# The first step of a state-space mixer, reordered: both row loads ahead of x's blocks, slot 4 ahead of the third scores, late step widths and softplus behind slot 5

## The reference

```python
proj = x @ W_in.T                       # val, gate, B, C for 32 heads, and dt (one number per head and token)
dt = softplus(dt + dt_bias)             # the "step width"
ld = dt * -exp(A_log)
cum = cumsum(ld, axis=time)
CB = einsum('blhn,bmhn->bhlm', C, B)    # scores
M = CB * exp(cum_l - cum_m) on and below the diagonal, else 0
Y = M @ val + D * val
Y = (Y * silu(gate)) @ W_out.T
```

## Time and profile before

| what | value |
|---|---|
| median of three runs | 763.05 us (760.58, 763.05, 763.11) |
| profiled execution, its time | 760.83 us |
| its span, first to last instruction | 759.0 us |
| PE busy | 729.5 us (96%), 5938 matmuls |
| DVE busy | 575.7 us (76%) |
| ACT busy | 450.5 us (59%) |
| POOL busy | 386.1 us (51%) |
| mean granted TensorE clock | 0.994 |

### The profile page before, as it was taken

How to read it: one execution, slowest core, us unless ns; L and a number is a source line. 1 busy time by engine, 2 the same in 40 slices (tenths; PEclk the granted TensorE clock), 3 DMA queues, 4 the chain that set the end, 5 groups by cost and what they waited for, 6 DMA issues and landing times. The chain is left out here.

```text
span 759.0 us, 17379 instructions
## 1 busy us (share of the span) xinstructions
PE 729.5 (96%) x5938; PEld 403.8 (53%) x5938; DVE 575.7 (76%) x1134; ACT 450.5 (59%) x885; POOL 386.1 (51%) x439
## 2 busy tenths in 40 slices
PE   8899999999999999999999999999889999989897
PEld 3455555565655556555565655556523333336454
DVE  5677867677686776858677687888778978986787
ACT  7844447645443764444486454555557876867676
POOL 2867627453363654435367693664402331359754
PEclk9999999999999999999999999999999999999999
DMA  6575233315422242522313322332041000000001
GB/s 208 193 213 181 62 56 55 89 46 124 142 55 61 50 108 47 160 86 55 80 43 98 86 71 66 73 79 35 1 180 47 24 15 23 23 1 2 29 29 57
DMA packets 34299, 57.92 MB, mean 76 GB/s; under 512 B 7056, under 2 KB 11920, under 8 KB 33680
## 3 DMA queue, kind: packets, MB, share of 16 engines
q1 hardware_dynamic: 33680, 57.08, 28.4%
q10 hardware_dynamic: 576, 0.31, 0.1%
HBM read 54.10 MB, written 2.36 MB: 74 GB/s over the span
## 5 line engine op out<-in xcount | busy, mean ns | idle before, releaser
L292 POOL TENSOR_TENSOR cum_rows<-cum_rows,cum_t 128x512 f32<-128x512 f32 x128 | 136.6, 1077 | 194.1 <-DMA cum_rows<-cum_scratch 194.1
L808 PE MATMUL pring<-xt_hi,w_hi 128*128 (+1 forms) x576 | 171.6, 380 | 0.0
L808 PE MATMUL pring<-xt_hi,w_lo 128*128 (+1 forms) x576 | 171.3, 379 | 0.0
L808 PE MATMUL pring<-xt_lo,w_hi 128*128 (+1 forms) x576 | 171.3, 379 | 0.0
L660 DVE TENSOR_TENSOR bt<-pring,bt 128x512 f16<-128x512 f32 x128 | 88.0, 688 | 72.0 <-ACT bt L449 71.9
L449 ACT CAST bt<-pring 128x512 f16<-128x512 f32 x128 | 74.6, 583 | 112.3 <-PE pring L808 112.1
L664 DVE TENSOR_TENSOR ct<-pring,ct 128x512 f16<-128x512 f32 x128 | 88.1, 689 | 54.2 <-ACT ct L453 53.9
L850 PEld LDWEIGHTS pscore<-ct,bt 128*128 128x128 f16 x1536 | 96.0, 98 | 34.4 <-issue 6.7
L850 PE MATMUL pscore<-ct,bt 128*128 128x128 f16 x1536 | 106.6, 219 | 3.6 <-DVE mt L632 2.2
L453 ACT CAST ct<-pring 128x512 f16<-128x512 f32 x128 | 74.8, 584 | 52.3 <-PE pring L808 52.2
L808 PEld LDWEIGHTS pring<-xt_hi,w_lo 128*128 128x128 f16 x576 | 56.4, 98 | 67.9
(11 more groups left out here) (166 smaller groups left out, 987.2 us busy)
## 6 DMA issues: line engine op xcount, KB each, us to landing
cum_rows<-cum_scratch SPq DMA_DIRECT2D x32, 1024.0 KB, 8.0
w_raw<-in_w_in SPq DMA_DIRECT2D x35, 256.0 KB, 6.4
q_rows<-in_xt SPq DMA_DIRECT2D x4, 512.0 KB, 10.4
acc<-in_x SPq DMA_DIRECT2D x1, 2048.0 KB, 7.6
vals<-in_vals SPq DMA_DIRECT2D x16, 128.0 KB, 2.0
out<-acc SPq DMA_DIRECT2D x7, 256.0 KB, 2.2
w_raw_e<-in_w_up SPq DMA_DIRECT2D x1, 1024.0 KB, 5.0
w_raw_e<-in_w_gate SPq DMA_DIRECT2D x1, 1024.0 KB, 7.2
```

Of the source, the lines that this page charges most:

```text
L292: nc.gpsimd.tensor_tensor(rows[:, par, :, q], rows[:, par, :, q], own, ALU.subtract).then_inc(sem("since"), 1)
L808: mm = nc.tensor.matmul(bank[name][:], w[:, c, k, cols], x[:, k, bass.ds(n % TB, 1), :].rearrange("p o n -> p (o n)"), start=(i == 0), sto ...
```

## The change

Four orders are changed, and no instruction is added or removed.

- SP: the second load of rows, `load_rows(0, 1, 1)`, moves in front of x's blocks 1 to 3. It still waits until the first has landed, so the three loads of x now wait for that too. The load of x in its other layout (`acc`, 2 MB) and of `expo` moves in front of `store_sums(1, TB)`, behind a new wait for W_out and the skip weights (`in_wo` at 32).
- PE: `pair(0, 4)` moves in front of `scores(0, 2)`. The three `step_widths` move from around `scores(0, 2)` to behind `pair(0, 5)`. `outputs(0, 0)` moves behind `pair(0, 6)`, in front of `scores(0, 5)`.
- ACT: the late `softplus` moves from in front of `evac_b(0, 4)` to behind `evac_c(0, 5)`, in front of `decays(0, 4)`.
- DVE: `low_b(0, 4)` and `low_c(0, 4)` move in front of `pad_values(0)`. The late `step_sizes` moves behind `low_c(0, 5)`, `rates` and `sums(1)` behind `weigh(0, 4)`, `sums(2)` and `sums(3)` behind `low_b(0, 6)` and `low_c(0, 6)`.

POOL's order is not touched.

```diff
@@ sync
             load_rows(0, 0, 0)
+            sp.wait_ge(sem("rows0"), 16)
+            load_rows(0, 1, 1)
             for t in range(1, TB):
                 load_x(t)
-            sp.wait_ge(sem("rows0"), 16)
-            load_rows(0, 1, 1)
             sp.dma_start(dskip[:], io["dskip"]).then_inc(sem("in_wo"), 16)
             sp.dma_start(wo, io["wo"]).then_inc(sem("in_wo"), 16)
+            sp.wait_ge(sem("in_wo"), 32)
+            sp.dma_start(acc[:], io["x"]).then_inc(sem("in_x"), 16)
+            sp.dma_start(expo[:], io["expo"]).then_inc(sem("in_x"), 16)
             sp.wait_ge(sem("dt_cum"), TB)
             store_sums(1, TB)
-            sp.dma_start(acc[:], io["x"]).then_inc(sem("in_x"), 16)
-            sp.dma_start(expo[:], io["expo"]).then_inc(sem("in_x"), 16)
             sp.wait_ge(sem("cum_out"), 32)
@@ scalar, first_step
                 for e in range(3):
                     decays(0, e)
-                act.wait_ge(sem("dt_mm"), TB)
-                softplus(slice(L, TOK), 3)
                 evac_b(0, 4)
                 evac_c(0, 4)
                 decays(0, 3)
                 evac_b(0, 5)
                 evac_c(0, 5)
+                act.wait_ge(sem("dt_mm"), TB)
+                softplus(slice(L, TOK), 3)
                 decays(0, 4)
@@ vector, first_step
                 weigh(0, 0)
                 weigh(0, 1)
+                low_b(0, 4)
+                low_c(0, 4)
                 pad_values(0)
                 weigh(0, 2)
-                step_sizes(slice(L, TOK), 3)
-                rates(slice(L, TOK), 3)
-                sums(1)
-                low_b(0, 4)
-                sums(2)
-                low_c(0, 4)
-                sums(3)
                 weigh(0, 3)
                 low_b(0, 5)
                 low_c(0, 5)
+                step_sizes(slice(L, TOK), 3)
                 weigh(0, 4)
+                rates(slice(L, TOK), 3)
+                sums(1)
                 low_b(0, 6)
+                sums(2)
                 low_c(0, 6)
+                sums(3)
                 weigh(0, 5)
@@ tensor, first_step
                 scores(0, 1)
                 pair(0, 3)
-                step_widths(1)
-                step_widths(2)
+                pair(0, 4)
                 scores(0, 2)
                 turn_values(0)
-                step_widths(3)
-                for s in range(4, SLOTS):
-                    pair(0, s)
-                    scores(0, s - 1)
-                    if s == 5:
-                        pe.wait_ge(sem("dt_log"), 4)
-                        pe.wait_ge(sem("dt_z"), 3)
-                        outputs(0, 0)
+                scores(0, 3)
+                pair(0, 5)
+                for t in range(1, TB):
+                    step_widths(t)
+                scores(0, 4)
+                pair(0, 6)
+                pe.wait_ge(sem("dt_log"), 4)
+                pe.wait_ge(sem("dt_z"), 3)
+                outputs(0, 0)
+                scores(0, 5)
+                pair(0, 7)
+                scores(0, 6)
                 turn_sums(1, TB)
```

## The result

The changed kernel takes 767.66 us (median of four executions, 766.99 to 768.7) against 763.08 us (four, 760.58 to 763.17): a ratio of 1.0069, with a 95% interval of 1.0045 to 1.0094. It is slower by 4.6 us by the medians. The ratios in this document are worked out from all executions and not from the medians (those alone would give 1.0060); the means stand 5.3 us apart (767.75 and 762.48). Timed again later beside other kernels (experiment 5), the ratio was 1.0097 [1.0072, 1.0123]. The profiled execution took 767.12 us, with a span of 765.3 us.

What follows compares the result with a forecast made beforehand. PE has no slack before 520 us, so delay in the late step-width thread arrives whole: a 4.8 us loss on 760.83 gives 765.6, on the median 763.05 gives 767.9; middle 766.5 us, range 762.3 to 770.

Steps and rivals of the forecast that it cites:

- What bounds the kernel: PE is busy from 110 to 520 us, so a delay in step 0 or 1 arrives at the end whole.
- SP and PE up to 41 us: Step 0: second rows land at 28.3 to 29.5 us; PE done by 41.3 with what it now does by 43.9.
- DVE and the scans: Step 0: POOL's 2.13 us subtractions hold two scans; store at 46.1 us, lower bound 43.6.
- The first stall: PE, free at 41.3 us, waits 4.5 us at `scores(0, 6)` for C's low part; step 1 starts at 46.8.
- The rows: Step 1's first rows: issued at 48.5 us, landed 8.0 later at 56.5 to 56.7 (load 7.7 to 9.2).
- From the decay to `out_project`: Step 1: first decay at 59.4 us, then 3.8 to 5.1 us, so `out_project` at 63.2 to 64.5 against 59.02.
- The median: Whole program: 765.6 us from the profiled execution, 767.9 from the median, the middle taken: 766.5 us.
- Not held up: Rival: scans pass POOL's work freely, store at 43.6 us, loss of 2.3 to 2.5 us; chance 0.26.
- The clock falls: Rival: PE drops to 1.2 GHz after the new stalls, 1.6 us more, 6.4 us loss, 768.1 us; chance 0.14.
- The thread is not the bound: Rival: step widths to step 1's rows not limiting; loss 0 or a gain, needs store before 42; chance 0.10.
- The rows in the queue: Rival: step 1's rows wait in the queue; slowest load 11.8 us behind `acc`, held to 9.2; no separate chance.
- the credit given for that edit: SP: `acc`, issued near 35 us, is gone before the store, so store and rows travel without it.

Runs made afterwards that it cites:

- experiment 5: The changed kernel timed once more, unchanged, beside other kernels: 769.1 us, ratio 1.0097 to the kernel before.
- experiment 7: Changed kernel with the late Ln, `rates` and scans working in PSUM, POOL's order kept: 766.16 us, ratio 1.0050 to the kernel before.
- experiment 3: Changed kernel with the 2 MB load of `acc` back behind the store of the sums: 771.19 us, ratio 1.0130 to the kernel before.
- experiment 4: Changed kernel with step 1's first rows and their own sums taken from block 0's early stored sums: 764.44 us, ratio 1.0033 to the kernel before.
- slot-4 order: Kernel before with `pair(0, 4)` ahead of `scores(0, 2)`, late softplus kept early: ratio 1.0041; 0.9993 with POOL's chunks 7 and 8 and `acc` also ahead.
- experiment 9: Kernel before with `pair(0, 4)` ahead, softplus kept early, POOL's chunks 7 and 8 ahead of `exponents(0, 1)`, `acc` directly behind W_out: 761.08 us, ratio 0.9993.
- 12: Experiment 9 with the late Ln, `rates` and scans in PSUM as well: 757.75 us, ratio 0.9946 to the kernel before.
- experiment 1: Changed kernel with POOL's x split for step 1 and W_out low part held until the scans are done: 764.99 us, ratio 1.0042 to the kernel before.
- experiment 2: Changed kernel with x's blocks 1 to 3 ahead of the second rows again: 768.26 us, ratio 1.0094 to the kernel before.
- 11: Kernel before, order untouched, with only the late Ln, `rates` and scans in PSUM: 759.42 us, ratio 0.9959.

## Why the prediction was right, point by point

- **What bounds the kernel.** Right: the delay of 6.43 us at 65 us is 6.42 at the last `out_project`. The steady part neither takes nor gives anything.
- **SP and PE up to 41 us.** Right within half a microsecond: second rows at 29.76 (28.3 to 29.5), x's last block let its step widths start at 33.54 (33.1 to 33.7; two waits for x, 1.07 us together, where the text had one of 0.4), Abs at 34.25 (33.8), fourth decay at 38.53 (38.1), `rates` at 39.86 (39.4). `scores(0, 2)` started at 26.71, not 27.1, in an execution whose projections also began 0.4 us earlier. POOL's long work began at 38.52 for 38.4, but by two errors that cancel: the rows came later than the range, and `exponents(0, 1)` took 8.8 us and not 9.4.
- **DVE and the scans.** The end was right and the assignment wrong. The text let `rates` through and had two scans held; `rates` and the first scan were held. The sum is the same two whole instructions of POOL, so the store went at 46.30 for 46.1. Which DVE instruction is held, and for how long, changes with the execution (`rates` 2.32 and 1.38 us in the two profiles of the kernel after); the end changes little, 46.30 and 46.65, since it follows the end of POOL's second subtraction. That the holds and no other thing make it is shown by experiment 7, where the same overlap without the second SBUF operand puts the store at 42.97.
- **The first stall.** 4.12 us for 4.5 (3.17 in the second profile). Step 1 began at 47.92 for 46.8: the scores and transposes took 1.87 us instead of 1.0, because the clock was at 0.50 by then. This hides in the second stall, as the text said.
- **The rows.** Here the sum was mis-sized. Issued at 48.84 (48.5), they took 9.1 us to POOL's start and not 8.0: landed at 57.9 for 56.6. The text took the median of 32 loads; this one has step 1's second rows directly behind it, and the 9.2 that the text kept as upper end was the better term. In the nine profiles with `acc` out of the way and the second rows behind, it is 8.7 to 9.1 us; that the second rows make it so is not tested. From the decay to `out_project` it was 4.86 us, inside 3.8 to 5.1 (the terms as listed add up to 3.6 to 4.9). Together 65.45 for 63.2 to 64.5, so the profiled loss is 6.3 where 4.8 was taken and 5.5 was the end.
- **The median.** 767.66 for 766.5, inside the range. The text had put it on the middle of two pairs of executions; the 4.6 us between the medians are smaller than the 6.3 between the profiles, because the execution profiled before was a short one (760.83 for 763.08). That 4.8 was taken and 4.6 measured is therefore luck in part: the means differ by 5.3 us, and like for like, the profiles differ by 6.3 us, more than the 5.5 at the upper end of the sum. The second set, +7.9 us, is a loss beyond the text's largest, 7 us, though its 769.1 us lies inside the range; its profile has the clock fall in it, and 6.4 us was the text's sum with that fall.
- **The rivals.** "Not held up" is experiment 7, and its price was 3.1 us at `out_project` and 0.5%, 3.8 us, in time, where 2.3 to 2.5 was worked out. "The clock falls" happens in some executions of the kernel after, at 1.75 us where 1.6 was worked out. "The thread is not the bound" needed a store before 42; it went at 46.30. The rows in the queue took less than 9.2 us, not 11.8. With `acc` put back (experiment 3) they took 11.3, so the credit given for that edit was right.

How the loss divides: of the 6.43 us, 3.3 go with the holds (experiment 7) and 3.1 are left without them; these go with the later place of the thread, which no run tests by itself. Cut the other way, 3.1 us go with step 1's rows being later than step 1's own work (experiment 4), and the other 3.35 us with the late start of step 1 and the half clock behind it. The gain was real: PE had its slot 7 projected by 41.9 us, about 2 us ahead of before, 0.4 of them from the earlier start of that execution. It was handed over to a wait for the low part of C, which stood in DVE's queue behind the scans.

## What to carry to other kernels

Filling the longest visible wait of the busiest engine moves time only if the thread behind it doesn't move later: here 1.5 of 2.2 us of PE idle were won by delaying softplus, scans, store and load, which had almost no slack to give. Before moving a vector operation, look at what the neighbour on the shared SBUF port does at the new time, for it waits out the other's whole instruction, and a short operation placed in front of the low parts makes PE wait as long. If it can't be moved away, put one of its operands in PSUM: that alone made the kernel before some 0.4% faster (0.15 to 0.66% by the interval) and turned the slot-4 order from no gain into 0.54%.

## What the runs showed of the hardware

- A scan and a two-input operation of DVE in SBUF are held until POOL's subtraction ends (2.23 us for 0.41, 2.32 for 0.61), and a subtraction that begins while `rates` is still running is itself stretched (2.44 for 2.13). With one operand in PSUM neither happens (0.42, 0.62 and 2.13 us).
- A DVE operation with a single tensor input, SBUF to SBUF in fp32, is held as well: 1.91 and 1.32 us for 0.47 (experiments 9, 12 and 7). The Trainium skill, "SBUF — State Buffer", Who interferes with whom, names this kind among those that may take both ports; the trace agrees, and the text on the scans had not counted it.
- The same stall of PE is followed by 1.2 GHz in one execution and by full clock in the next, with ends within 0.4 us of each other. Its length doesn't decide it: the clock fell behind stalls of 1.94 us (experiment 9), 2.01 (experiment 1) and 2.18 (experiment 2, at `scores(0, 6)`), and stayed at 1.00 behind 2.91 and 3.17 us (the two profiles of the kernel after). A fall is worth 1.75 us behind the second stall, 1.7 us behind the first where the rows don't hide it (experiment 4), and 1.2 us or so where the attention begins (212.3 us from the last `out_project` to the end against 211.1).
- The 1 MB load of rows takes 9.1 us to POOL's start with another one behind it (kernel after, experiment 7) and 11.3 with 2 MB ahead of it as well (experiments 3 and 11), against 8.0 in the median of before.
